# Local attention on one Trainium2 core: probabilities divided on GpSimd ahead of their transposition, value products written feature-major, attended rows no longer transposed

## What is computed

```python
h = shift_token(x)
q, k, v = jnp.split(h @ wqkv, 3, axis=-1)          # 8 heads of 64 features each
q = l2norm(q) * qs
k = l2norm(k) * ksc
q, k = rotary_xpos(q, k)
# each window of 64 queries sees its own window and the one before it
sim = jnp.einsum('bhwid,bhwjd->bhwij', bq * 8.0, look_around(bk))
sim = jnp.where((i < j) | (i > j + WINDOW) | (j == -1), -big, sim)
attn = jax.nn.softmax(sim, axis=-1)
out = jnp.einsum('bhwij,bhwjd->bhwid', attn, look_around(bv))
x = x + out.reshape(b, n, 512) @ wo
```

## Time and profile before

| | |
|---|---|
| median of 3 runs | 3182.64 us (3181.36 to 3185.25) |
| the profiled execution's own time | 3200.86 us |
| its span on the core | 3198.5 us |
| busy share, PE / PEld | 90 % / 56 % |
| busy share, DVE / ACT / POOL | 66 % / 65 % / 32 % |
| mean granted TensorE clock | 0.952 of full speed |
| steady part of local attention, layer 1 (2424 to 3008 us) | PE busy 575.2, DVE 470.0, ACT 500.0, POOL 308.5 of 584 us, granted clock 1.00 |

### The profile page before, as it was taken

The page is one execution under the profiler, slowest core; times in us unless marked ns, Lnnn a source line. Parts: engine busy times, 40 slices in busy tenths (PEclk is TensorE's granted clock), DMA queues, the critical chain, the costliest instruction groups (busy, mean ns, idle before and its releaser), DMA issues. The chain is left out here.

```text
span 3198.5 us, 64445 instructions
## 1 busy us (share of the span) xinstructions
PE 2880.4 (90%) x19916; PEld 1802.6 (56%) x19916; DVE 2125.0 (66%) x3261; ACT 2075.9 (65%) x5545; POOL 1011.4 (32%) x1162
## 2 busy tenths in 40 slices
PE   6899899996989779848799999998988999999899
PEld 3577896763744334425456666665435666666543
DVE  4566555655844579646668787875436888788556
ACT  3456565556733744243278888886867888888686
POOL 0233343320000024100055555553215555555321
PEclk9799998998989889889889999999998999999999
DMA  4200220000000000120000000000000000000000
GB/s 133 73 20 20 57 64 17 20 17 4 1 8 1 0 15 1 52 31 1 17 2 0 0 0 0 0 0 8 1 18 1 0 0 0 0 0 0 8 20 33
DMA packets 82860, 51.48 MB, mean 16 GB/s; under 512 B 28720, under 2 KB 75440, under 8 KB 82736
## 3 DMA queue, kind: packets, MB, share of 16 engines
q1 hardware_dynamic: 78640, 41.56, 4.6%
q0 software_dynamic: 4096, 8.40, 0.9%
HBM read 31.59 MB, written 18.35 MB: 16 GB/s over the span
## 5 line engine op out<-in xcount | busy, mean ns | idle before, releaser
L1835 PE MATMUL banks<-wqkv,hf 128*128 128x512 f32 x768 | 438.7, 655 | 37.1 <-POOL hf L335 24.6
L1959 ACT ACTIVATE probs<-banks,minus_max,rnorm 128x128 f32<-128x128 f32 x1024 | 454.8, 465 | 3.1 <-DVE minus_max L2044 3.1
L1869 POOL TENSOR_TENSOR qk_cross<-qk_raw,rope_scaled 128x512 f32<-128x512 f32 x256 | 325.4, 1272 | 50.7 <-DVE minus_max L2044 32.8
L2024 DVE COPY probs_t<-banks 128x512 f32<-128x512 f32 x256 | 176.1, 688 | 135.1 <-PE banks L1813 134.2
L1959 ACT ACTIVATION_READ_ACCUMULATOR probs<-banks,minus_max,rnorm 128x1 f32 x1024 | 218.9, 214 | 0.0
L707 ACT ACTIVATE probs<-banks,minus_max 128x128 f32<-128x128 f32 (+1 forms) x512 | 207.9, 425 | 16.1 <-DVE minus_max L746 14.6
L1879 POOL TENSOR_TENSOR qk_rot<-qk_rot,rnorm 128x512 f32<-128x512 f32 x128 | 133.4, 1042 | 260.4 <-DVE qk_rot L2077 247.3
L2040 DVE TENSOR_REDUCE minus_raw<-banks 128x8 f32<-128x1024 f32 x128 | 156.7, 1225 | 56.8 <-PE banks L1800 32.4
L1827 PE MATMUL banks<-v_tok,probs_t 128*64 128x64 f32 x3072 | 174.6, 228 | 9.0 <-DVE probs_t L2024 3.8
L1827 PEld LDWEIGHTS banks<-v_tok,probs_t 128*64 128x64 f32 x3072 | 139.2, 137 | 71.8 <-issue 42.5
L2058 DVE TENSOR_REDUCE sumsq<-qk_sq 128x16 f32<-128x1024 f32 x128 | 154.8, 1209 | 27.0 <-issue 19.9
(11 more groups left out here) (339 smaller groups left out, 7053.2 us busy)
## 6 DMA issues: line engine op xcount, KB each, us to landing
sorted_x<-zero_rows SPq DMA_DIRECT2D x10, 512.0 KB
rows_in<-sorted_x SPq DMA_DIRECT2D x18, 256.0 KB, 3.2
sorted_y<-rows_out SPq DMA_DIRECT2D x18, 256.0 KB, 2.4
x_res<-in_x SPq DMA_DIRECT2D x8, 512.0 KB, 6.5
out_x<-x_res SPq DMA_DIRECT2D x16, 256.0 KB, 2.0
w1b<-in_L_ffn_w SPq DMA_DIRECT2D x8, 256.0 KB
s_branch<-in_L_ffn_w SPq DMA_DIRECT2D x8, 256.0 KB
w1g<-in_L_ffn_W SPq DMA_DIRECT2D x8, 256.0 KB, 3.0
```

Source lines behind the costliest of these rows:

```text
L1835: pe.matmul(ps[:, misc(k, j)], hf[:, n // 2 % 2, 0, n % 2 * P:(n % 2 + 1) * P], wqkv[:, w:w + QW], start=True, stop=True).then_inc(*S[name ...
L1869: return pool.tensor_tensor(by_half(tw[:, n, at]), by_half(qk[:, n, at])[:, :, ::-1, :], tab[:, n, 2 * w + 1].rearrange("p (a d) -> p a d" ...
L1959: last = act.activation(pr[:, k % 2, head], ps[:, 2 * (k % 2) + par, c * P:(c + 1) * P], ACT.Exp, scale=rn[:, k % 4, head:head + 1], bias= ...
L2024: dve.tensor_copy(pt[:, h], ps[:, 4]).then_inc(*S["turned_sb"].inc)
```

## The change

- The row sums are inverted on VectorE by half (`inverse`, four heads at a time, into a two-block buffer), and GpSimd multiplies the probabilities of each head, 128x128 in place, by the inverse of their row (`weigh`, L1883 of the changed kernel). Turn 0 and turn 1 wait for this instead of for the exps.
- The value products have the values as their stationary side and the turned probabilities as their moving side, so that bank 5 receives feature-major rows: even heads on partitions 0 to 63, odd heads on 64 to 127. Even blocks have one product of 128 columns per head, odd blocks two of 64.
- The transposes of the attended rows and ScalarE's copy of them are gone. VectorE copies bank 5 into `ot` where it made the attended product.
- The output product is of block k-2, behind the v projection, and the residual add goes to the end of VectorE's slot. `MISC` has six entries for seven.

```diff
-MISC = [("qt_sb", 1), ("added", -3), ("q_sb", 3), ("kt_sb", 1), ("k_sb", 3), ("v_sb", 1), ("ot_sb", -2)]
-QT_AT, OUT_AT, Q_AT, KT_AT, K_AT, V_AT, OT_AT = range(7)
+MISC = [("qt_sb", 1), ("q_sb", 3), ("kt_sb", 1), ("k_sb", 3), ("v_sb", 1), ("added", -2)]
+QT_AT, Q_AT, KT_AT, K_AT, V_AT, OUT_AT = range(6)
...
-        sums, rs = buf("row_sums", P, 2, HEADS), buf("inv_sums", P, HEADS)
-        o, ot = buf("attended_tok", P, QW), buf("ot", P, 4, P)
+        sums, rs = buf("row_sums", P, 2, HEADS), buf("inv_sums", P, 2, HEADS)
+        ot = buf("ot", P, 4, P)
...
         def pe_turn(pe, i, k, h):
-            pe.wait_ge(*S["exps"].at(i, 2 * k + h))
+            pe.wait_ge(*S["weighed"].at(i, 2 * k + h))
             pe.wait_ge(*S["turned_sb"].at(i, 2 * k + h - 1))
             for n in range(4):
                 mm = pe.transpose(ps[:, 4, n * P:(n + 1) * P], pr[:, k % 2, 4 * h + n], m["ident"][:])
             tb = k % 2
             pe.wait_ge(*S["turned_sb"].at(i, 2 * k + h))
             if h == 0:
-                pe.wait_ge(*S["attended"].at(i, k - 1))
+                pe.wait_ge(*S["ot_sb"].at(i, k - 1))
                 pe.wait_ge(*S["v_sb"].at(i, k))
                 if tb:
                     pe.wait_ge(*S["v_mixed"].at(i, k // 2))
+            width = P // (1 + tb)
             for n in range(4):
-                at = slice((4 * h + n) * DH, (4 * h + n + 1) * DH)
-                for w in range(2):
-                    mm = pe.matmul(ps[64 * w:64 * w + 64, 5, at], pt[:, h, n * P + 64 * w:n * P + 64 * w + 64],
-                                   vm[:, at] if tb and not w else va[:, k % 4, at], start=True, stop=True)
+                head = 4 * h + n
+                at = slice(head * DH, (head + 1) * DH)
+                rows = slice(head % 2 * 64, head % 2 * 64 + 64)
+                for w in range(1 + tb):
+                    first = head // 2 * P + w * width
+                    mm = pe.matmul(ps[rows, 5, first:first + width],
+                                   vm[:, at] if tb and not w else va[:, k % 4, at],
+                                   pt[:, h, n * P + w * width:n * P + (w + 1) * width], start=True, stop=True)
             mm.then_inc(*S["mixed"].inc)
...
+                def weigh(i, k, h):
+                    pool.wait_ge(*S["rowsum"].at(i, 2 * k + h))
+                    pool.sem_inc(S["g3"].sem, 1)
+                    for head in range(4 * h, 4 * h + 4):
+                        last = pool.tensor_scalar(pr[:, k % 2, head], pr[:, k % 2, head], rs[:, k % 2, head:head + 1], None,
+                                                  ALU.mult)
+                    last.then_inc(*S["weighed"].inc)
                 def slot(i, k):
...
                         cross(i, k, 0)
+                    if here(i, k - 1):
+                        weigh(i, k - 1, 1)
+                    if here(i, k + 2):
                         if here(i, k):
                             pool.wait_ge(*S["rowmax"].at(i, k))
                         cross(i, k, 1).then_inc(*S["crossed"].inc)
...
+                        if here(i, k - 1):
+                            pool.wait_ge(*S["weighed"].at(i, 2 * (k - 1) + 1))
...
+                        if here(i, k - 1):
+                            pool.wait_ge(*S["weighed"].at(i, 2 * (k - 1) + 1))
                         shift_in(pool, hf[:, k // 2], m["xn"], i, 0, T, S["v_ps"].at(i, k + 1), first=first)
...
-                rounds_of(pool, R, 1, 0, lambda i: [slot(i, k) for k in range(4)])
+                    if here(i, k):
+                        weigh(i, k, 0)
+                rounds_of(pool, R, 1, 1, lambda i: [slot(i, k) for k in range(4)])
...
                     if here(i, k + 1):
                         pe_turn_qk(pe, i, k, QT_AT, "qt")
-                    if here(i, k - 3):
-                        pe_free(pe, i, k, OUT_AT)
-                        pe.wait_ge(*S["ot_sb"].at(i, k - 3))
-                        for c in range(4):
-                            mm = pe.matmul(ps[:, misc(k, OUT_AT), 0:P], wo[:, c], ot[:, c], start=(c == 0), stop=(c == 3))
-                        mm.then_inc(*S["o_ps"].inc)
                     if here(i, k + 3):
                         pe_project(pe, i, k, k + 3, Q_AT, "q")
...
                     if here(i, k - 2):
-                        pe_free(pe, i, k, OT_AT)
-                        pe.wait_ge(*S["attended"].at(i, k - 2))
+                        pe_free(pe, i, k, OUT_AT)
+                        pe.wait_ge(*S["ot_sb"].at(i, k - 2))
                         for c in range(4):
-                            mm = pe.transpose(ps[:, misc(k, OT_AT), c * P:(c + 1) * P], o[:, c * P:(c + 1) * P],
-                                              m["ident"][:])
-                        mm.then_inc(*S["ot_ps"].inc)
+                            mm = pe.matmul(ps[:, misc(k, OUT_AT), 0:P], wo[:, c], ot[:, c], start=(c == 0), stop=(c == 3))
+                        mm.then_inc(*S["o_ps"].inc)
                     if here(i, k - 1):
                         pe_mix(pe, i, k - 1, 1)
...
-                    if here(i, k - 2):
-                        act.wait_ge(*S["ot_ps"].at(i, k - 2))
-                        act.wait_ge(*S["o_ps"].at(i, k - 3))
-                        act.activation(ot[:], bank(ps, misc(k, OT_AT), 4, P), ACT.Copy).then_inc(*S["ot_sb"].inc)
                     if here(i, k):
                         exps(i, k, 1)
...
+                def inverse(i, k, h):
+                    heads = slice(4 * h, 4 * h + 4)
+                    dve.wait_ge(*S["exps"].at(i, 2 * k + h))
+                    dve.wait_ge(*S["weighed"].at(i, 2 * (k - 2) + h))
+                    dve.reciprocal(rs[:, k % 2, heads], sums[:, k % 2, heads]).then_inc(*S["rowsum"].inc)
                 def slot(i, k):
                     if here(i, k - 2):
-                        dve.wait_ge(*S["exps"].at(i, 2 * (k - 2) + 1))
-                        dve.reciprocal(rs[:], sums[:, k % 2]).then_inc(*S["rowsum"].inc)
-                        dve.wait_ge(*S["rowsum"].at(i, k - 2))
                         dve.wait_ge(*S["mixed"].at(i, 2 * (k - 2) + 1))
-                        dve.wait_ge(*S["ot_ps"].at(i, k - 3))
-                        dve.tensor_tensor(by_head(o[:]), bank(ps, 5, HEADS, DH),
-                                          rs[:].unsqueeze(2).to_broadcast([P, HEADS, DH]), ALU.mult)\
-                            .then_inc(*S["attended"].inc)
+                        dve.wait_ge(*S["o_ps"].at(i, k - 3))
+                        dve.tensor_copy(ot[:], bank(ps, 5, 4, P)).then_inc(*S["ot_sb"].inc)
...
-                    if here(i, k - 3):
-                        xn = m["xn"][:, bass.ds((i * 4 + k - 3) * P, P)]
-                        dve.wait_ge(*S["o_ps"].at(i, k - 3))
-                        dve.wait_ge(S["first"].sem, PRIME)
-                        dve.tensor_tensor(xn, xn, ps[:, misc(k, OUT_AT), 0:P], ALU.add).then_inc(*S["added"].inc)
+                    if here(i, k - 1):
+                        inverse(i, k - 1, 1)
                     if here(i, k - 1):
                         turned(i, k - 1, 0)
...
+                    if here(i, k):
+                        inverse(i, k, 0)
                     if here(i, k - 1):
                         turned(i, k - 1, 1)
                     if here(i, k + 2):
                         dve.wait_ge(*S["straight"].at(i, k + 2))
                         dve.wait_ge(*S["crossed"].at(i, k + 2))
                         dve.tensor_tensor(st[:, n], st[:, n], tw[:, n % 2], ALU.add).then_inc(*S["rotated"].inc)
+                    if here(i, k - 2):
+                        xn = m["xn"][:, bass.ds((i * 4 + k - 2) * P, P)]
+                        dve.wait_ge(*S["o_ps"].at(i, k - 2))
+                        dve.wait_ge(S["first"].sem, PRIME)
+                        dve.tensor_tensor(xn, xn, ps[:, misc(k, OUT_AT), 0:P], ALU.add).then_inc(*S["added"].inc)
```

More of the change, by code:

```diff
@@ L1848, in local_attention @@
                              "rnorm", "crossed", "rotated", "unit", "qt_ps", "kt_ps", "qt_sb", "kt_sb", "scores",
-                             "rawmax", "rowmax", "rowsum", "attended", "ot_ps", "ot_sb", "o_ps", "added"], 4)
-        per.update(copied=2, v_mixed=2, g2=2, exps=8, turned=8, turned_sb=8, mixed=8)
+                             "rawmax", "rowmax", "ot_sb", "o_ps", "added"], 4)
+        per.update(copied=2, v_mixed=2, g2=2, g3=8, exps=8, rowsum=8, weighed=8, turned=8, turned_sb=8, mixed=8)
         with Stage(R, **per), nc.Block() as block:
@@ L1953, in exps @@
                     act.wait_ge(*S["turned"].at(i, 2 * (k - 2) + h))
-                    if h == 0:
-                        act.wait_ge(*S["rowsum"].at(i, k - 2))
+                    act.wait_ge(*S["rowsum"].at(i, 2 * (k - 2) + h))
                     for n in range(4):
```

## The result

The changed kernel took 3441.7 us (median of 4 runs, 3440.4 to 3449.0) against 3182.0 us before: a ratio of 1.083, interval 1.082 to 1.085. It is slower by 260 us. The forecast was slower by 76 us, 3258, in a range that ended at 3330.

What follows compares the result with a forecast made beforehand. VectorE and GpSimd holding each other up were to set slots of 10.0 us against 9.39; 124 slots give + 76 us, less 18 from the profiled 3277 to the median: 3258 us, range 3160 to 3330.

Steps and rivals of the forecast that it cites:

- the price of the division: GpSimd's eight 128x128 multiplications per slot: 0.332 us each taken, between 0.294 and 0.447, 2.7 us a slot.
- an estimated 0.19 us: Price of one 128-element GpSimd multiplication by the skill's cycle accounting; would make the sum of two slots 17.8, not 20.0.
- Rival B: GpSimd weighing costs 0.447 or more: 10.9 us a slot, 3374 us; sign: GpSimd gapless, turn 1 waiting; chance 0.08.
- The sum of what runs one after the other: GpSimd's and VectorE's mutually exclusive work over two slots: 14.7 us before, 20.0 after, so 10.0 us a slot.
- The hold: VectorE and GpSimd: one holds their port pair exclusively for a whole instruction, whoever comes first; without it 9.24 us slots.
- The forecast's rule from four rows: A VectorE operation with two SBUF inputs, or the clamp, and any GpSimd operation here run one after the other.
- ScalarE's loop: ScalarE's copies gate the k and v projections; with everything else hidden, v at 5.03 behind F and a 9.24 us slot.
- only 0.15 of 0.73 us would be left: TensorE's removed transposes take 0.73 us a slot, wait included; with everything else hidden, 0.15 remains as gain.
- VectorE's loop: VectorE's reduction, copies, clamp and rope products lead to the second copy of turned probabilities, for which mix 1 waits.
- Rival D: ScalarE's loop gives way too and the whole 0.73 us is saved: -91 us, 3092 us, slots under 9; chance 0.05.
- the mix bound: Odd-block mixes on TensorE running one by one: + 0.3 us per mix, upper bound 0.15 us a slot, 19 us in all.
- The mixes: TensorE's value products in their new form: extra cost taken as nothing, since four heads still alternate between the halves.

Runs made afterwards that it cites:

- no division: Changed kernel without the eight multiplications, probabilities undivided, all waits kept, GpSimd only signals: ratio 0.993 to the kernel before.
- broadcast product: Changed kernel with one GpSimd product of 128x512 per half, inverses broadcast along the row, for the eight multiplications: ratio 1.000 to the kernel before.
- half of the multiplications: Changed kernel with only two of four heads of each half multiplied, the other probabilities undivided: ratio 1.006 to the kernel before.
- two operations: Changed kernel with an idle multiplication by 1.0 added to each multiplication's instruction, same result: 3236.9 us against 3197.6 for the kernel before.
- one of 128x512 per half: Changed kernel with one one-operation multiplication of 128x512 per half by the first head's scalar: 3266.6 us against 3196.1 for the kernel before.
- constant: Changed kernel with the eight multiplications by constant 0.125 instead of a scalar per partition, probabilities undivided: 3328.3 us against 3197.6 for the kernel before.
- the output product put back: Changed kernel without division, output product (block k-2) and residual add put back behind the q transposes: ratio 1.004 to the kernel before.

## Why the prediction was wrong

**The step that failed is the price of the division**: "A quarter of the extra ... gives 0.294 + 0.038 = 0.332, which I take", and with it the upper bound of 0.447. One measured 0.605 undisturbed. The nearest rows were of other forms: a copy, and a multiplication with two operations. The form with one operation costs 2.5 ns an element where those cost 0.83 and 1.03. Eight of them are 4.8 us a slot where 2.7 stood in the sum. Which property of the form makes it dear stays open: the runs show the price with a scalar, with a constant, with a second operation and with four times the elements, and no more. The rule that I cited from the Trainium skill, "GPSIMD Engine Reference", "Elementwise — side-by-side cycle accounting", gave an estimated 0.19 us; no multiplication of this size here came near it (0.371 to 0.605).

**What the wrong price did**, by the runs with other forms of the division; the division's time is per slot and undisturbed, the sum is the forecast's (GpSimd's own 9.2 + twice the division + VectorE's 5.5, over two):

| run | division, us | slot, us | sum, us |
|---|---|---|---|
| no division | 0 | 9.23 | 7.4 |
| broadcast product | 2.1 | 9.48 | 9.4 |
| half of the multiplications | 2.4 | 9.63 | 9.8 |
| two operations | 3.0 | 9.75 | 10.3 |
| one of 128x512 per half | 3.1 | 10.03 | 10.5 |
| constant | 4.2 | 10.45 | 11.6 |
| the change | 4.8 | 11.5 | 12.2 |

Up to 3.1 us the slot has grown by an eighth to a quarter of the division's time; from 4.2 to 4.8 it grows by 1.0 for 0.6. There GpSimd is the bound: busy 93 % of the stretch with the constant and 91 % with the change. Its multiplications took 0.576 and 0.695 in the mean against 0.528 and 0.605 undisturbed, so 0.95 us more a slot, of which 0.62 is their own time and 0.33 VectorE in the way. Of the 9 % that is left with the change, 0.5 us a slot is GpSimd's wait for the v projection before its shifted copies, and the v projection stands behind turn 1, which waits for the multiplications. All this is read from the two traces, not tested by a run of its own.

**Rival B** ("0.447 or more: 10.9 a slot") is the one that came true, beyond its own number, with a chance of 0.08. Its sign was there: turn 1 waiting for GpSimd, and GpSimd nearly without a gap.

**The sum of what runs one after the other** was right in kind and too strict. With the true price it gives 12.2, 0.7 too much. It hits the broadcast product, overstates every dearer form, and without division another loop decides. At 3.0 us of division, more than the 2.7 for which 10.0 was forecast, the slot measured 9.75, and the time was 39 us over the kernel before. So this is a second fault: with the price right, + 76 us would still have been about twice too much.

The hold itself is real, and for GpSimd's products of two tensors it agrees with the Trainium skill, "SBUF — State Buffer", section "Who interferes with whom": from 1650 to 2150 us each of the 28 `minus_max` that were issued while the k norm or a cross product ran ended 0.02 us behind it. Beside the multiplications it is weaker. The other 16, issued 0.25 to 0.51 us after the start of a multiplication, took 0.17 us as if nothing ran, like this one:

```profile
1705.30 0.60 POOL L1883 TENSOR_SCALAR probs<-probs,inv_sums 128x128 f32<-128x128 f32 x1
...
1705.56 0.17 DVE L2055 TENSOR_TENSOR minus_max<-minus_raw,rnorm 128x8 f32<-128x8 f32 x1
```

And in the slot shown above the clamp and two rope products lie within the four multiplications from 2908.41 on:

```profile
2909.04 0.34 DVE L2068 TENSOR_SCALAR sumsq<-sumsq 128x16 f32<-128x16 f32 x1
2909.39 1.29 DVE L2076 TENSOR_TENSOR qk_rot<-qk_raw,rope_scaled 128x512 f32<-128x512 f32 x2
```

VectorE's three take 0.17 + 1.29 undisturbed, the four multiplications 2.35 (as at 2903.83). One after the other that is 3.8 us; it took 3.25. So a multiplication of this form is not closed to VectorE for all of its 0.605 us, and the sum counted it as if it were. The forecast's rule from four rows, that any GpSimd operation here and VectorE's run one after the other, does not hold for it. How much of the difference this explains in the runs with other forms was not read.

**ScalarE's loop** was right, and not by luck: 9.23 for 9.24, with the k projection behind raw q, the v projection behind k^T, and v at 5.02 or 5.03 behind F in three slots of four. So was the reading that only 0.15 of 0.73 us would be left (0.20 measured). **VectorE's loop** as the next one was right in kind with the output product put back (9.6 expected for that run, 9.44 measured). Rival D, the whole 0.73, is refuted by both.

Two small terms were off and change nothing: a reciprocal of half the sums takes 0.17 us, so two of them add 0.14 to the old 0.20 and not 0.2; and a division of 0.39 us together with the mix bound comes to 3335, a little over the range's end of 3330 that was said to take them in.

**The mixes** at nothing: borne out by the broadcast product's ratio of 1.000 and the run without division, which met its forecast with that term at nothing. The timelines say it directly: from the start of a mix to the next group is 0.62 us before, and 0.59 (even blocks) or 0.66 (odd blocks) without division.

**The granted clock** was no part of the forecast. It fell to its lower level (1.2 GHz) for 3.4 us at a time, in one slot of two or three, after TensorE had stood still for 2.0 to 2.3 us in front of turn 1. Filling that wait brought it back, made the slots even and changed nothing in the time.

## What to carry to other kernels

Take the price of an instruction from a row of the same engine, operation count and operand kind, not only of the same size; where there is none, treat the term as open, and let its upper end hold the chance that the form is another one. Before work is moved to an idle engine, sum that engine's whole slot with the new work at twice its price: GpSimd's own 4.6 us and the forecast 2.7 leave room in a slot of 9.4, 4.6 and 4.8 leave none. And look for the loop that closes last: 0.18 us off VectorE's loop in the old kernel gained as much as 0.73 us off TensorE's with the division left out altogether.

## What the runs showed of the hardware that I had not expected

- GpSimd's multiplication of 128x128 float32 by a scalar per partition takes 0.605 us with one operation and 0.371 with a second, idle one; 128x512 takes 1.567 and 0.767. With a constant it is 0.528 for 128x128.
- One GpSimd product of 128x512 with the scalars broadcast takes 1.04 us, less than half of four single multiplications (2.42).
- VectorE's clamp of 128x16 took up to 1.31 us (run with one 128x512 multiplication; 0.17 undisturbed), held up by a GpSimd product of two tensors. A GpSimd fill was never held up (1.04 us in all 256 cases) and in the steady part held up nothing.
- A product of two tensors on VectorE, issued 0.25 us or more after the start of a one-operation multiplication on GpSimd, took 0.17 us as if alone; issued during a GpSimd product of two tensors it ended 0.02 us behind that.
- After a stand of 2.0 to 2.3 us TensorE's granted clock fell to its lower level for 3.4 us in one slot of two or three. Slots with a fall took 13.2 us in the mean, the others 10.5, and the mean (11.5) was nearly that of the run with the clock at 1.00 throughout (11.45). In all runs with slots up to 10.5 us the steady stretch kept 1.00.
